# Layer 2's rotary swap by transfers, odd-shaped row writes, a bias on GpSimd, input rows turned first

## The chip, the cores and the metric

The kernel runs on one core of a Trainium2 chip. The metric is the device time of one execution in microseconds. Beside the plain runs one execution was profiled; its trace gives the spans and durations below. Engines: PE is TensorE's matmuls and PEld its weight loads, DVE is VectorE, ACT is ScalarE, POOL is GpSimd, SP is SyncE (here it only issues transfers).

## The reference

A decoder of four layers on x of 128 sequences x 64 tokens x 128 features, float32, residual and layer norm after each block. The seven attention blocks that the change touches have 16 heads of 8 features each; L2's self-attention rotates q and k by halves (feature i is paired with feature i+64):

```python
def _rope(x, base=ROPE_BASE):
    half = D // 2
    x1, x2 = (x[..., :half], x[..., half:])
    return jnp.concatenate([x1 * cos - x2 * sin, x1 * sin + x2 * cos], axis=-1)
# every attention block: softmax(q k / sqrt(8) + mask) v, heads joined, then
# x = layernorm(x + o @ Wo + bo)
```

Between these blocks stand mixtures of experts, a grouped attention, a recurrent block and a channel mix, which the change leaves alone.

## The kernel before

One function, `attention` (line 254), writes seven stages: L0a (self), L0x (cross, rotated by rows), L1x (cross) with L1f (self) behind it, L2a (self) with L2x (cross) behind it, and L3x (cross). A stage that follows another uses its buffers and overlaps its end, so the trace names L1f's tiles L1x and L2x's tiles L2a. The residual rows X stay in SBUF. The work is cut into 32 pairs of tiles (256 rows each).

Each engine has a generator `slot(T)`, one per engine; `all_pairs` (line 156) runs it for T from -4 to 32 and some more, six slots unrolled, 22 in a loop, the rest unrolled. Within an engine the order is the order of the program; between engines `made` waits for a counter. In slot T the stages of work belong to different pairs: scores of T, probabilities and values of T-1, output of T-2, written rows of T-3, projections of T+2, input copy of T+3. L3x, which has a second layer norm in between (`ln_o`), has its output two pairs later.

- TensorE, `slot` at line 620: scores (L563 is the causal mask, L569 the products with KB), the two transposes of the attention output ON (L630), the two transposes of the input rows XS (`fill_turn`, L584), then transposes of the probabilities (L617) in four groups, with the k projection (`fill_projection`, L597, and L599 for the product with the swapped weights) and the q projection between them, the output projection (L672), probabilities times values (L683), and the value projection (`fill_v`, L609). All projections of a slot share the one PSUM bank psF.
- ScalarE, `slot` at line 706: copies the turned output (OT, L711), then the turned input (XT, L719; in L3x CX, L717), the probabilities (PT, L697), the projections (RK through `raw_parts`, L702 to L704, with a bias column; where nothing is rotated QK directly, L736 and L749), then the exponential (L756) and the values (VB, L771).
- VectorE, `slot` at line 777: reduction and subtraction over the scores (L781, L784, 2048 columns each), the normalized rows of pair T-3 into X (L805, one `tensor_scalar` of 128 columns for each of the two tiles; in L3x also OL, L797), the residual sum RB (L816), statistics, 1/sum, and ON (L848). In L0a and L3x it also multiplies the k part by the rotation table (L404).
- GpSimd, `slot` at line 445: the roots of the variances (rs, L459, L461), XR = X + bias row (L482, in the stages with `bias_row`), the copy XS (L498), and at the end the rotation of pair T+2: product with the table (L404), sum of the two parts into KT (L524), the same for q into QT (L529). In L0x its own work is the rotation by rows (L416 to L428), and the bias is added on TensorE (L670, a product of the identity with the broadcast row).
- SP, `slot` at line 349: loads, and four transfers (L385) of the finished keys KT of pair T+2 into KB, after `k_roped`.

For rotation, RK holds for k and for q the projection (columns 0 to 255) and the projection by swapped weights (256 to 511); the product with cosine and sine tables and a sum make the rotated rows. Features are ordered so that the swap by halves is a swap of partitions 0 to 63 with 64 to 127. `pace` adds one to a semaphore that nobody waits for; it is a marker instruction in front of another.

Of the kernel before, what the change touches and what calls it, by code (L numbers as in the profile page):

```python
# [176 lines left out]
def build(nc, io, out):  # L177
    ctx = ExitStack()
    with ctx:
# [74 lines left out]
        def attention(L, q, k, v, o, qs=None, ks=None, bq=None, bqs=None, bk=None, bks=None, bo=None,  # L254
# [5 lines left out]
            turned = ks is not None  # L260
# [13 lines left out]
            RK = mem.sb("RK", [P, 2, 512]) if turned else None  # L274
# [41 lines left out]
            bias_on_pe = by_rows  # L316
            bias_row = rowx[:, 0, :] if ln_o else None if bias_on_pe else bo
# [30 lines left out]
            def sync(sp):  # L348
                def slot(T):
# [29 lines left out]
                    if K.ok:  # L379

                        made(sp, "k_roped" if turned else "o_k", K.p + 1)
                        pace(sp, S)
                        made(sp, "scores", K.p - 1)
                        for b in range(HQ):
                            sp.dma_start(KB[b:P:HQ, K.u, b, :, :].rearrange("p s k -> p (s k)"), KT[b:P:HQ, K.u, :]).then_inc(parity_sem("keys_in", K), 16)  # L385
# [15 lines left out]
            def rope_product(eng, n, tab):  # L401

                parts = RK[:, n].rearrange("p (c s k) -> p c s k", c=2, s=4)
                return eng.tensor_tensor(parts, parts, rope[:, tab:tab + 2, :].unsqueeze(2).to_broadcast([P, 2, 4, SEQ]), ALU.mult)  # L404

            def gpsimd(g):
# [37 lines left out]

                def slot(T):
# [9 lines left out]
                    if F.ok:  # L455

                        made(g, "stats", F.p + 1)
                        made(g, "out_rows", F.p - 1)
                        nc.gpsimd.tensor_tensor(rs[:, F.u, 0, :], mv[:, F.u, :, 1], eps[:, 0:2], ALU.add).then_inc(S["var_eps"].sem, 1)  # L459
                        made(g, "var_eps", F.p + 1)  # L460
                        nc.gpsimd.tensor_tensor(rs[:, F.u, 1, :], rs[:, F.u, 0, :], half[:, 0:2], ALU.pow).then_inc(S["rstd"].sem, 1)  # L461
                        if not rows_on_dve:
                            nc.gpsimd.tensor_tensor(RB[:, F.u], RB[:, F.u], mv[:, F.u, :, 0:1].to_broadcast([P, 2, D]), ALU.subtract).then_inc(S["mix"].sem, 1)
                            made(g, "rstd", F.p + 1)
                            made(g, "mix", F.p + 1)
                            pace(g, S)
                            nc.gpsimd.tensor_tensor(rows_of(F), RB[:, F.u], rs[:, F.u, 1, :].unsqueeze(2).to_broadcast([P, 2, D]), ALU.mult).then_inc(S["out_rows"].sem, 1)
                    A = T - 2
# [47 lines left out]
                    M = T + 2  # L516
                    if turned and M.ok:

                        if not products_on_dve:
                            made(g, "o_k", M.p + 1)  # L520
                            rope_product(nc.gpsimd, 0, ck).then_inc(S["gates"].sem, 1)
                        made(g, "gates", M.p + 1)
                        parity_wait(g, "keys_in", M - 2, 16 * HQ)
                        nc.gpsimd.tensor_tensor(KT[:, M.u], RK[:, 0, 0:256], RK[:, 0, 256:512], ALU.add).then_inc(S["k_roped"].sem, 1)  # L524
                        made(g, "o_q", M.p + 1)
                        rope_product(nc.gpsimd, 1, cq).then_inc(S["gates_out"].sem, 1)
                        made(g, "gates_out", M.p + 1)
                        made(g, "scores", M.p - 1)
                        nc.gpsimd.tensor_tensor(QT[:, M.u], RK[:, 1, 0:256], RK[:, 1, 256:512], ALU.add).then_inc(S["q_roped"].sem, 1)  # L529
# [8 lines left out]
            def tensor(pe):  # L538
# [81 lines left out]
                def slot(T):  # L620
# [3 lines left out]
                    yield  # L624
                    if H.ok:
# [6 lines left out]
                    yield  # L632
                    if N.ok and not by_rows:
                        fill_turn(N)
# [28 lines left out]
                    if H.ok:  # L663
# [5 lines left out]
                        if bias_on_pe:  # L669
                            nc.tensor.matmul(psJ, ident, bo.unsqueeze(1).to_broadcast([P, 2, D]), start=True, stop=False, skip_group_check=True)  # L670
                        for a in range(2):
                            m = nc.tensor.matmul(psJ[:, a, :], OT[:, H.u, a * P:a * P + P], o, start=not bias_on_pe, stop=True, skip_group_check=bias_on_pe)  # L672
# [20 lines left out]
            def scalar(act):  # L693
# [5 lines left out]
                def raw_parts(n, biases):  # L699

                    if biases[0] is None:
                        return nc.scalar.activation(RK[:, n, :], psF[:, :], ACT.Copy)  # L702
                    nc.scalar.activation(RK[:, n, 0:256], psF[:, 0:256], ACT.Identity, bias=biases[0])
                    return nc.scalar.activation(RK[:, n, 256:512], psF[:, 256:512], ACT.Identity, bias=biases[1])  # L704

                def slot(T):
                    A, N, H = T - 1, T + 2, T - 2 - e
                    if H.ok:
                        made(act, "o_turned", H.p + 1)
                        made(act, "proj", H.p - 1)  # L710
                        nc.scalar.activation(OT[:, H.u, :], flat(psOT), ACT.Copy).then_inc(S["ot"].sem, 1)  # L711
                    yield
                    if N.ok and not by_rows:
# [4 lines left out]
                        else:  # L718
                            nc.scalar.activation(XT[:, N.u, :], psF[:, 0:256], ACT.Copy).then_inc(S["o_tx"].sem, 1)  # L719
                    yield  # L720
# [4 lines left out]
                    if N.ok:  # L725
# [5 lines left out]
                        elif turned:  # L731
                            made(act, "k_roped", N.p)
                            raw_parts(0, (bk, bks)).then_inc(S["o_k"].sem, 1)
# [8 lines left out]
                    if N.ok and not by_rows:  # L742
                        made(act, "f_q", N.p + 1)
                        if turned:
                            made(act, "q_roped", N.p)
                            raw_parts(1, (bq, bqs)).then_inc(S["o_q"].sem, 1)
# [29 lines left out]
            def vector(dv):  # L776
                def slot(T):
# [9 lines left out]
                    if turned and products_on_dve and M.ok:  # L787
                        made(dv, "o_k", M.p + 1)
                        rope_product(nc.vector, 0, ck).then_inc(S["gates"].sem, 1)
                    yield  # L790
                    B = T - 3
                    if ln_o and B.ok:
# [3 lines left out]
                        for a in range(2):  # L796
                            m = nc.vector.tensor_scalar(OL[:, B.u, a, :], ON[:, B.u, a, :], mvo[:, B.u, a, 0:1], rso[:, B.u, 1, a:a + 1], ALU.subtract, ALU.mult)  # L797
# [65 lines left out]
            count(dict.fromkeys(("q_roped", "k_roped", "gates_out", "gates"), PAIRS), turned)  # L863
            count(dict(side_made=1, w_in0=32 * PAIRS, w_in1=32 * PAIRS), mask is by_key)
# [1520 lines left out]
        def grouped_attention(later):  # L2385
# [72 lines left out]
            with nc.Block() as block:  # L2458
# [135 lines left out]
                def _(dv):  # L2594
# [78 lines left out]
        turning = attention("L2a", Wm("L2q"), Wm("L2k"), Wm("L2v"), Wm("L2o"), qs=Wm("L2qs"), ks=Wm("L2ks"), bq=C("L2bq"), bqs=C("L2bqs"),  # L2673
                  bk=C("L2bk"), bks=C("L2bks"), bo=rowb[:, 2, :], cq=2, ck=2, mask=static)
# [128 lines left out]
```

## Time and profile before

| | us |
|---|---|
| median of 3 runs | 4016.08 (4015.06 to 4021.43) |
| profiled execution | 4011.83 |
| its span, first to last instruction | 4010.0 |
| PE busy | 3481.2 (87%) |
| DVE busy | 2993.7 (75%) |
| ACT busy | 2291.8 (57%) |
| POOL busy | 1885.8 (47%) |

The shares are averages over stages with different limits; the mean granted TensorE clock is 0.933 of full speed. Attention stages lie at about 12 to 330 us (L0a), 337 to 610 (L0x), 1557 to 2090 (L1x, L1f), 2392 to 2970 (L2a, L2x) and 3521 to 3884 (L3x). In views of waits a row says who waited for whom, the total in us, how often, and the longest. In views in order of time a row has the start, the time to the end, engine, line, operation, output and inputs, the count, and in brackets the idle time before it and who ended that.

### The profile page before, as it was taken

How to read it: one execution, taken by the hardware profiler on the slowest of the kernel's cores; microseconds unless marked ns; L12 is line 12 of the kernel's file. 1: busy time of each engine (PE TensorE's matmuls, PEld its weight loads, DVE VectorE, ACT ScalarE, POOL GpSimd, SP SyncE). 2: the span in 40 equal slices, each digit the busy share in tenths (PEclk: the TensorE clock that was granted, in tenths of full speed). 3: DMA queues.
4: the chain of work that ended last, by engine and by line, in shares of the span. 5: the costliest groups of instructions: out<-in, count | busy, mean ns of one | idle time of the engine just before them, and what ended most of it. 6: DMA issues, size and time to landing. Idle time of an engine off the chain costs nothing. (4 is left out here: it accounts for less than half of the span.)

```text
span 4010.0 us, 127677 instructions
## 1 busy us (share of the span) xinstructions
PE 3481.2 (87%) x46840; PEld 2654.2 (66%) x46840; DVE 2993.7 (75%) x6186; ACT 2291.8 (57%) x3920; POOL 1885.8 (47%) x2970
## 2 busy tenths in 40 slices
PE   8996996797999998999987839999989688879985
PEld 6885775465777776878875627778854254457764
DVE  6986995155898886888863477888867588659975
ACT  5775771344444444778752447777754466556653
POOL 6887864655441111224545436652223355457754
PEclk9997995899999998999986969999989799989988
DMA  2002213697000000110005820001112000000001
GB/s 82 29 27 80 69 54 103 180 262 196 19 16 3 0 0 29 50 49 19 17 19 155 240 70 16 14 25 53 49 42 65 23 0 0 1 26 27 26 8 42
DMA packets 311910, 219.08 MB, mean 55 GB/s; under 512 B 52689, under 2 KB 290257, under 8 KB 311505
## 3 DMA queue, kind: packets, MB, share of 16 engines
q1 hardware_dynamic: 251824, 166.57, 14.3%
q0 software_dynamic: 12288, 25.19, 2.0%
q10 hardware_dynamic: 47520, 23.60, 2.0%
q8 instruction: 177, 2.90, 0.3%
q14 instruction: 101, 0.82, 0.1%
HBM read 131.27 MB, written 54.53 MB: 46 GB/s over the span
## 5 line engine op out<-in xcount | busy, mean ns | idle before, releaser
L781 DVE TENSOR_REDUCE L2a_mx<-L2a_psS 128x32 f32<-128x2048 f32 x64 | 146.7, 2292 | 75.8 <-PE L2a_psS L569 75.8
L781 DVE TENSOR_REDUCE L1x_mx<-L1x_psS 128x32 f32<-128x2048 f32 x64 | 146.7, 2292 | 74.5 <-PE L1x_psS L569 74.5
L2474 POOL TENSOR_TENSOR L1a_rs<-L1a_ag,eps 128x1 f32<-128x1 f32 x64 | 13.0, 204 | 397.8 <-DVE L1a_ag L2639 397.8
L1111 POOL DMA_INDIRECT L0f_sorted_x<-X,L0f_IDX x128 | 123.0, 961 | 93.8 <-DMA L0f_sorted_x<-X,L0f_IDX 35.6
L1530 DVE TENSOR_TENSOR L0f_G<-L0f_SG,L0f_psH 128x512 f32<-128x512 f32 x106 | 73.0, 689 | 120.1 <-ACT L0f_SG L1274 72.7
L459 POOL TENSOR_TENSOR L1x_rs<-L1x_mv,eps 128x2 f32<-128x2 f32 x64 | 12.5, 195 | 310.5 <-DVE L1x_mv L836 310.5
L784 DVE TENSOR_TENSOR L2a_PR<-L2a_psS,L2a_mx 128x2048 f32<-128x2048 f32 x64 | 146.7, 2292 | 7.3
L784 DVE TENSOR_TENSOR L1x_PR<-L1x_psS,L1x_mx 128x2048 f32<-128x2048 f32 x64 | 146.7, 2292 | 7.3 <-DVE L1x_mx L781 0.2
L697 ACT ACTIVATE L2a_PT<-L2a_psP 128x512 f32<-128x512 f32 x256 | 146.0, 598 | 2.9 <-PE L2a_psP L617 1.4
L697 ACT ACTIVATE L1x_PT<-L1x_psP 128x512 f32<-128x512 f32 x256 | 145.9, 595 | 3.0 <-PE L1x_psP L617 1.4
L617 PE MATMUL L1x_psP<-W,L1x_PR 128*128 128x128 f32 x1024 | 146.9, 277 | 0.2
L617 PE MATMUL L2a_psP<-W,L2a_PR 128*128 128x128 f32 x1024 | 145.7, 276 | 0.2
L756 ACT ACTIVATE L1x_PR<-L1x_PR 128x2048 f32<-128x2048 f32 x64 | 122.3, 1912 | 37.0 <-DVE L1x_PR L784 37.0
L2563 PE MATMUL L1a_psO<-rest_WO,L1a_OT 128*64 128x128 f32 x2048 | 125.9, 276 | 11.5 <-ACT L1a_OT L2588 7.4
L756 ACT ACTIVATE L2a_PR<-L2a_PR 128x2048 f32<-128x2048 f32 x64 | 122.6, 1915 | 18.5 <-DVE L2a_PR L784 18.5
L617 PEld LDWEIGHTS L1x_psP<-W,L1x_PR 128*128 128x128 f32 x1024 | 118.0, 142 | 20.7 <-ACT L1x_PT L697 13.9
L617 PEld LDWEIGHTS L2a_psP<-W,L2a_PR 128*128 128x128 f32 x1024 | 120.0, 142 | 17.6 <-ACT L2a_PT L697 7.9
L683 PE MATMUL L1x_psB<-VB,L1x_PT 128*64 128x18 f32 x4096 | 131.4, 212 | 0.0
L2497 PE MATMUL L1a_psF<-L1a_XT,rest_WQ 128*128 128x256 f32 x512 | 131.0, 390 | 0.5 <-DVE L1a_KT L2449 0.5
L2563 PEld LDWEIGHTS L1a_psO<-rest_WO,L1a_OT 128*64 128x64 f32 x2048 | 110.5, 137 | 31.4 <-ACT L1a_OT L2588 31.3
L683 PE MATMUL L2a_psB<-VB,L2a_PT 128*64 128x18 f32 x4096 | 131.2, 212 | 0.0
L683 PEld LDWEIGHTS L1x_psB<-VB,L1x_PT 128*64 128x64 f32 x4096 | 125.0, 138 | 7.8 <-issue 0.4
(624 smaller groups left out, 11625.1 us busy)
## 6 DMA issues: line engine op xcount, KB each, us to landing
L0f_WB<-in_w12a SPq DMA_DIRECT2D x53, 312.0 KB, 3.8
L0f_XB<-L0f_sorted_x SPq DMA_DIRECT2D x53, 256.0 KB, 4.0
L0f_sorted_y<-L0f_YB ACTq DMA_DIRECT2D x53, 256.0 KB, 3.8
L1m_WB<-in_w12b SPq DMA_DIRECT2D x37, 321.0 KB, 4.1
L1m_XB<-L1m_sorted_x SPq DMA_DIRECT2D x37, 256.0 KB, 4.0
L1m_sorted_y<-L1m_YB ACTq DMA_DIRECT2D x37, 256.0 KB, 4.4
L0x_VS<-in_ctx SPq DMA_DIRECT2D x64, 128.0 KB, 2.7
KB<-L1x_QK SPq DMA_DIRECT2D x256, 32.0 KB, 1.8
```

What stands on the lines that cost most here:

```text
L459: nc.gpsimd.tensor_tensor(rs[:, F.u, 0, :], mv[:, F.u, :, 1], eps[:, 0:2], ALU.add).then_inc(S["var_eps"].sem, 1)
L617: m = nc.tensor.transpose(psP[:, bank, n, :], PR[:, A.u, r, b:b + 2, :].rearrange("p h k -> p (h k)"), ident)
L683: m = nc.tensor.matmul(psB[64 * s:64 * s + 64, (j * HP + b) * VW:(j * HP + b + 1) * VW], PT[:, j, b, 64 * s:64 * s + 64], VB[:, A.u, 2 * j ...
L697: nc.scalar.activation(PT[:, j, 4 * hb:4 * hb + 4, :], psP[:, bank], ACT.Copy).then_inc(S["pt_a"].sem, 1)
L756: nc.scalar.activation(PR[:, T.u], PR[:, T.u], ACT.Exp, scale=scale).then_inc(S["probs"].sem, 1)
L781: nc.vector.tensor_reduce(mx[:, T.u, :], sc, AX, ALU.max).then_inc(S["maxed"].sem, 1)
L784: nc.vector.tensor_tensor(PR[:, T.u].rearrange("p r h k -> p (r h) k"), sc, mx[:, T.u, :].unsqueeze(2).to_broadcast([P, 2 * HEADS, SEQ]), ...
L1111: nc.gpsimd.indirect_dma_start(out=sorted_x[p][:, :], out_offset=bass.IndirectOffsetOnAxis(ap=IDX[:, k, t:t + 1], axis=0), in_=X[:, t, :], ...
L1530: nc.vector.tensor_tensor(G[0:f, J % 2, c, :], SG[0:f, c, :], up, ALU.mult).then_inc(S["g_ready"].sem, 1)
L2474: nc.gpsimd.tensor_tensor(rs[:, A.par, 0:1], ag[:, A.par, 1:2], eps[:, 0:1], ALU.add).then_inc(S["var_eps"].sem, 1)
L2497: m = nc.tensor.matmul(bank[:, 256 * j:256 * j + 256], WQ[:, 2 * k + j, :], XT[:, N.u, :], start=True, stop=True)
L2563: m = nc.tensor.matmul(psJ[64 * s:64 * s + 64, :], OT[:, s, c, :], WO[:, s, c, :], start=c == 0, stop=c == QC - 1, skip_group_check=True)
```

## The change

1. L2a is called with `halves=True` and without swapped weights and swapped biases. ScalarE copies only the straight projection (256 columns) of k and of q into RK, which now has two buffers. SP, after both copies, issues two transfers of 64 partitions each that write the swapped halves of k and q together. GpSimd's rotation, now `rotate(M)`, waits for them (`stored`), works on pair T+1 instead of T+2, and stands behind the roots rather than at the end of its slot. SP's key transfers follow it: pair T+1 in L2a, in front of the swap of T+2.
2. The bias of L0x goes from TensorE to XR on GpSimd.
3. In all stages but L0x TensorE does `fill_turn` ahead of the transposes of the output, and ScalarE copies the turned input ahead of OT.
4. Each row write on VectorE (L805, and OL in L3x) becomes two, of columns 0 to 62 and 63 to 127, with an output of 7x9 against an input of 3x21, and 13x5 against 5x13.
5. ScalarE issues a marker (`pace`) in front of the raw copies of L0a, L2a and L3x.

```diff
+                    B = T + ahead if turned else K
+                    if B.ok:
+                        made(sp, "k_roped" if turned else "o_k", B.p + 1)
                         pace(sp, S)
+                        made(sp, "scores", B.p - 1)
                         for b in range(HQ):
+                            sp.dma_start(KB[b:P:HQ, B.u, b, :, :].rearrange("p s k -> p (s k)"), KT[b:P:HQ, B.u, :]).then_inc(parity_sem("keys_in", B), 16)
+                    if halves and K.ok:
+                        made(sp, "o_k", K.p + 1)
+                        pace(sp, S)
+                        made(sp, "o_q", K.p + 1)
+                        for n in range(2):
+                            here, there = slice(64 * n, 64 * n + 64), slice(64 - 64 * n, 128 - 64 * n)
+                            sp.dma_start(RK[here, K.u, :, 256:512], RK[there, K.u, :, 0:256]).then_inc(parity_sem("stored", K), 16)
...
+                def rotate(M):
+                    if turned and M.ok:
+                        if not products_on_dve:
+                            if halves:
+                                parity_wait(g, "stored", M, 32)
+                            else:
+                                made(g, "o_k", M.p + 1)
+                            rope_product(nc.gpsimd, M, 0, ck).then_inc(S["gates"].sem, 1)
+                        made(g, "gates", M.p + 1)
+                        parity_wait(g, "keys_in", M - 2, 16 * HQ)
+                        nc.gpsimd.tensor_tensor(KT[:, M.u], RK[:, kept(M), 0, 0:256], RK[:, kept(M), 0, 256:512], ALU.add).then_inc(S["k_roped"].sem, 1)
...
+                    if halves:
+                        rotate(T + 1)
                     A = T - 2
...
+                    if not halves:
+                        rotate(T + 2)
...
                         scores(T)
                     yield
+                    if N.ok and not by_rows:
+                        fill_turn(N)
+                    yield
                     if H.ok:
...
-                        if bias_on_pe:
-                            nc.tensor.matmul(psJ, ident, bo.unsqueeze(1).to_broadcast([P, 2, D]), start=True, stop=False, skip_group_check=True)
...
+                    if halves:
+                        return nc.scalar.activation(RK[:, N.u, n, 0:256], psF[:, 0:256], ACT.Identity, bias=biases[0])
...
+                def scaled_rows(dst, rows_, mean, root):
+                    for lo, hi, x, y in ((0, 63, 7, 3), (63, D, 13, 5)):
+                        m = nc.vector.tensor_scalar(dst[:, lo:hi].rearrange("p (x y) -> p x y", x=x), rows_[:, lo:hi].rearrange("p (x y) -> p x y", x=y), mean, root, ALU.subtract, ALU.mult)
+                    return m
...
-                            m = nc.vector.tensor_scalar(xo, RB[:, F.u, a, :], mv[:, F.u, a, 0:1], rs[:, F.u, 1, a:a + 1], ALU.subtract, ALU.mult)
+                            m = scaled_rows(xo, RB[:, F.u, a, :], mv[:, F.u, a, 0:1], rs[:, F.u, 1, a:a + 1])
```

## Rows read from the trace of the kernel before

**Rows 1.** Score reductions by tile: count, min/median/max ns, first and last start.

```profile
L781 DVE TENSOR_REDUCE L0a_mx<-L0a_psS x32: 2291/2292/2294, 29.9 to 308.1; 128x32 f32<-128x2048 f32 x32
...
L781 DVE TENSOR_REDUCE L0x_mx<-L0x_psS x32: 2280/2291/2292, 353.0 to 589.7; 128x32 f32<-128x2048 f32 x32
...
L781 DVE TENSOR_REDUCE L1x_mx<-L1x_psS x64: 2291/2292/2294, 1570.7 to 2066.4; 128x32 f32<-128x2048 f32 x64
...
L781 DVE TENSOR_REDUCE L2a_mx<-L2a_psS x64: 2291/2292/2293, 2411.0 to 2946.7; 128x32 f32<-128x2048 f32 x64
...
L781 DVE TENSOR_REDUCE L3x_mx<-L3x_psS x32: 2280/2292/2294, 3542.7 to 3856.2; 128x32 f32<-128x2048 f32 x32
```

**Rows 2.** Windows of L0a, L0x, L3x: us, then PE, PEld, DVE, ACT, POOL busy, clock.

```profile
60.00:290.00 230.00, 225.73 (x4098) 189.44 (x4096) 207.06 (x358) 164.58 (x281) 193.09 (x398) 1.00 0.09 29
380.00:580.00 200.00, 181.78 (x3249) 153.35 (x3247) 194.12 (x288) 149.57 (x235) 173.22 (x306) 1.00 0.23 68
...
3580.00:3830.00 250.00, 237.82 (x3645) 186.35 (x3637) 234.68 (x431) 173.44 (x315) 185.33 (x291) 1.00 0.08 26
```

**Rows 3.** Waits in stretches of L0a, L1f, L3x: total us, times, longest us.

```profile
DVE L0a_mx L781 <- PE L0a_psS L569: 17.3, 25, 0.9
...
DVE L1x_mx L781 <- PE L1x_psS L569: 19.7, 26, 0.8
...
DVE L3x_mx L781 <- PE L3x_psS L569: 12.3, 23, 1.8
```

**Rows 4.** One slot of L2a in order of time.

```profile
2529.97 2.29 DVE L781 TENSOR_REDUCE L2a_mx<-L2a_psS 128x32 f32<-128x2048 f32 x1 [0.87 <-PE L2a_psS L569]
...
2530.32 0.38 ACT L711 ACTIVATE L2a_OT<-L2a_psP 128x256 f32<-128x256 f32 x1 [1.00 <-PE L2a_psP L630]
...
2530.60 0.38 ACT L719 ACTIVATE L2a_XT<-L2a_psF 128x256 f32<-128x256 f32 x1
...
2531.03 0.30 PEld L597 LDWEIGHTS L2a_psF<-L2a_XT,W 128*128 128x128 f32 x2 [0.41 <-ACT L2a_XT L719]
...
2531.57 0.60 PE L599 MATMUL L2a_psF<-L2a_XT,W 128*128 128x256 f32 x2
...
2532.00 1.04 PE L617 MATMUL L2a_psP<-W,L2a_PR 128*128 128x128 f32 x8
...
2533.17 0.30 PEld L597 LDWEIGHTS L2a_psF<-L2a_XT,W 128*128 128x128 f32 x2 [0.37 <-ACT L2a_RK L704]
...
2533.20 1.27 POOL L404 TENSOR_TENSOR L2a_RK<-L2a_RK,rope 128x512 f32<-128x512 f32 x1 [2.32 <-ACT L2a_RK L704]
...
2534.62 1.99 DVE L805 TENSOR_SCALAR X<-L2a_RB,L2a_mv,L2a_rs 128x128 f32 x2
...
2539.31 2.29 DVE L781 TENSOR_REDUCE L2a_mx<-L2a_psS 128x32 f32<-128x2048 f32 x1 [1.04 <-PE L2a_psS L569]
```

**Rows 5.** Transfers of the whole trace: KB each, median us to landing.

```profile
L0x_VS<-in_ctx SPq DMA_DIRECT2D x64, 128.0 KB, 2.7
...
KB<-L2a_QK SPq DMA_DIRECT2D x256, 32.0 KB, 1.8
```

**Rows 6.** VectorE in order of time in L1x: a pair of row writes.

```profile
1702.18 0.60 DVE L805 TENSOR_SCALAR X<-L1x_RB,L1x_mv,L1x_rs 128x128 f32 x2
1702.69 0.42 DVE L816 TENSOR_TENSOR L1x_RB<-L1x_psP,L1x_XR 128x256 f32<-128x256 f32 x1
```

**Rows 7.** Groups of instructions by line and shape: busy us, mean ns.

```profile
L482 POOL TENSOR_TENSOR L2a_XR<-X,rowb 128x256 f32<-128x256 f32 x64 | 47.5, 742 | 0.0
...
L805 DVE TENSOR_SCALAR X<-L3x_RB,L3x_mv,L3x_rs 128x128 f32 x44 | 34.6, 826 | 0.0
L805 DVE TENSOR_SCALAR X<-L0x_RB,L0x_mv,L0x_rs 128x128 f32 x44 | 33.1, 791 | 0.0
...
L797 DVE TENSOR_SCALAR L3x_OL<-L3x_ON,L3x_mvo,L3x_rso 128x128 f32<-128x128 f32 x64 | 31.1, 528 | 2.7 <-POOL L3x_rso L453 2.7
...
L805 DVE TENSOR_SCALAR X<-L0a_RB,L0a_mv,L0a_rs 128x128 f32 x44 | 20.4, 504 | 0.0
```

More of the change, by code:

```diff
@@ L251, in build, with attention @@
         S.advance(dict(zeroed=1))
-        def attention(L, q, k, v, o, qs=None, ks=None, bq=None, bqs=None, bk=None, bks=None, bo=None,
+        def attention(L, q, k, v, o, qs=None, ks=None, bq=None, bqs=None, bk=None, bks=None, bo=None, halves=False,
                       cq=0, ck=0, cross=False, norm=None, mask=None, ln_o=False, affine=None, keep=None, tally=False, arrive=False, tables=None, follows=None):
@@ L259, in attention @@
             by_rows = tables is not None
-            turned = ks is not None
+            turned = ks is not None or halves
+            ahead = 1 if halves else 2
             turn_c = cross and norm is not None and not by_rows
@@ L273, in attention @@
             RA = mem.sb("RA", [P, 2, 2, 2 * P]) if by_rows else None
-            RK = mem.sb("RK", [P, 2, 512]) if turned else None
+            RK = mem.sb("RK", [P, 2, 2, 512]) if turned else None
             QK = mem.sb("QK", [P, 2, 2, 2 * P])
@@ L443, in mean_squares @@
                     nc.gpsimd.tensor_scalar(dst, Q1[:, n, :], 1.0 / HD, RMS_EPS, ALU.mult, ALU.add).then_inc(S[done].sem, 1)
+                def rotate(M):
[10 more added lines that the diff above has]
+                        if halves:
+                            parity_wait(g, "stored", M, 32)
+                        else:
+                            made(g, "o_q", M.p + 1)
+                        rope_product(nc.gpsimd, M, 1, cq).then_inc(S["gates_out"].sem, 1)
+                        made(g, "gates_out", M.p + 1)
+                        made(g, "scores", M.p - 1)
+                        nc.gpsimd.tensor_tensor(QT[:, M.u], RK[:, kept(M), 1, 0:256], RK[:, kept(M), 1, 256:512], ALU.add).then_inc(S["q_roped"].sem, 1)
                 def slot(T):
@@ L515, in slot @@
                         mean_squares(N.p, CS[:, N.u], 0, MC[:, N.u, :], "stat_root", "means")
[L516 to L529, printed above, removed]
+                    if not halves:
+                        rotate(T + 2)
                     Y = T - 4
@@ L668, in slot @@
                             made(pe, "res", H.p)
[L669 to L670 removed]
                         for a in range(2):
[L672 removed]
+                            m = nc.tensor.matmul(psJ[:, a, :], OT[:, H.u, a * P:a * P + P], o, start=True, stop=True)
                         m.then_inc(S["proj"].sem, 1)
@@ L731, in slot @@
                         elif turned:
-                            made(act, "k_roped", N.p)
-                            raw_parts(0, (bk, bks)).then_inc(S["o_k"].sem, 1)
+                            made(act, "k_roped", N.p - 1 if halves else N.p)
+                            pace(act, S)
+                            raw_parts(N, 0, (bk, bks)).then_inc(S["o_k"].sem, 1)
                         else:
@@ L744, in slot @@
                         if turned:
-                            made(act, "q_roped", N.p)
-                            raw_parts(1, (bq, bqs)).then_inc(S["o_q"].sem, 1)
+                            made(act, "q_roped", N.p - 1 if halves else N.p)
+                            pace(act, S)
+                            raw_parts(N, 1, (bq, bqs)).then_inc(S["o_q"].sem, 1)
                         else:
@@ L863, in attention @@
             count(dict.fromkeys(("q_roped", "k_roped", "gates_out", "gates"), PAIRS), turned)
+            count(dict(stored0=16 * PAIRS, stored1=16 * PAIRS), halves)
             count(dict(side_made=1, w_in0=32 * PAIRS, w_in1=32 * PAIRS), mask is by_key)
@@ L2671, in build @@
         keep.close()
-        turning = attention("L2a", Wm("L2q"), Wm("L2k"), Wm("L2v"), Wm("L2o"), qs=Wm("L2qs"), ks=Wm("L2ks"), bq=C("L2bq"), bqs=C("L2bqs"),
-                  bk=C("L2bk"), bks=C("L2bks"), bo=rowb[:, 2, :], cq=2, ck=2, mask=static)
+        turning = attention("L2a", Wm("L2q"), Wm("L2k"), Wm("L2v"), Wm("L2o"), halves=True, bq=C("L2bq"),
+                  bk=C("L2bk"), bo=rowb[:, 2, :], cq=2, ck=2, mask=static)
         run(turning, attention("L2x", Wm("L2xq"), Wm("L2xk"), Wm("L2xv"), Wm("L2xo"), bq=C("L2xbq"), bk=C("L2xbk"), bo=rowb[:, 3, :], cross=True, follows=turning))
```

39 lines of the change are left out of this document (17 added, 22 removed).

## The prediction

> **What bounds the kernel now.** I first read how long one slot (one pair of tiles) takes in each attention stage: the first and the last start of the score reduction, divided by the slots between [rows 1]. L0a 8.97 us, L0x 7.64, L1x with L1f 7.87, L2a with L2x 8.50, L3x 10.11. Next the busy time in a steady stretch [rows 2]: TensorE is busy 225.73 of 230 us in L0a, but 181.78 of 200 in L0x, where VectorE has 194.12. In L3x both are near 94% (237.82 and 234.68 of 250). Then the waits [rows 3]: VectorE's reduction waits for TensorE's scores 17.3 us in 25 slots of L0a (0.69 each), 19.7 in 26 of L1f (0.76), and 12.3 us in about 25 slots of L3x (0.49). So TensorE's program order is the bound in L0a, L1, L2 and L3x, with VectorE 0.5 to 1.0 us behind it, and VectorE is the bound in L0x. The granted clock is 1.00 (2.4 GHz) in these stretches. Last, one slot of L2a in order of time [rows 4]: 9.34 us from one reduction to the next, with two holes in TensorE's weight loads, 0.41 us for the copy of the turned input rows and 0.37 us for the copies of the key halves.
>
> **Layer 2 swap by transfers.** Removed on TensorE, in each of L2a's 32 slots: two projections by swapped weights (ks, qs). One takes 0.43 us of order (L599 starts at 2531.57, the next work at 2532.00) [rows 4], so 0.86. Removed on ScalarE: the second copy of each, which starts the q projection 0.37 us late; with that copy gone the transposes in front (to 2533.04) cover it, so 0.37 more. Added: two transfers of 128 KB each on SP's queue, issued after both copies; in SP's program order they stand behind the four key transfers of the pair before. GpSimd's rotation (product 1.27 us, add about 0.73, twice: 4.0) now waits for these transfers, and runs one slot later and at the head of GpSimd's slot, ahead of the residual's bias add and the input copy. Behind its wait are queued XR (VectorE's residual sum waits for that) and XS. No row shows a partition-crossing swap of this size; the nearest is L0x's pair of 128 KB loads, 2.7 us to landing, and the small end is the key transfers, 1.8 [rows 5]. I take 2.7. Slack, counted from the slot's reduction: the q projection starts at 3.2 today (2533.17), so at 2.0 without those 0.41, 0.43 and 0.37; with its 0.70 and the ScalarE copies in front of its own the q copy ends at about 3.5. I estimate that the next slot's rotation can begin 0.3 before that slot's reduction, so in a slot of P us a swap of up to P-3.8 costs nothing. After the rotation XR ends at -0.3+4.0+0.74 = 4.4; VectorE wants it after its row writes, 4.65 (2534.62) + 1.02 = 5.7: 1.2 more. At P=7.9 the swap may take 5.3. Keys leave at 1.7, land by 4.4, and scores want them some 2 us before the next reduction, at 5.9. So the swap is hidden.
> The Trainium skill, DMA: Bandwidth & Descriptors, Rules for kernel authors, speaks against two transfers to the two halves of the partitions, since they serialize. That would mean double the 1.8 us at worst, an estimate of 3.6, still under 5.3, so the sum would be the same. No run here yet shows it.
>
> **Input rows ahead of the turned output.** In all stages but L0x, TensorE turns the input rows before the attention output, and ScalarE copies them before OT. The order of work is otherwise the same. The hole of 0.41 us exists since ScalarE's OT copy starts at 2530.32 and XT's at 2530.60 [rows 4]; now XT goes first, 0.28 us sooner, and its transpose 0.17 sooner. The k projection gains up to 0.41, at least 0: the copy chain PT, k copy, PT on ScalarE may not follow. What becomes late next is OT, by 0.3 us, wanted by the second group of transposes only. In L0a and L3x a marker instruction is added ahead of each of the two raw copies; no row prices it on ScalarE, I take 0.02 to 0.07 each. I take a net 0.27 a slot for TensorE in L0a and L3x, and let VectorE decide elsewhere. The new order makes the slot's first TensorE work wait for the value copy of the slot before; ScalarE ends that just before today's slots do, so little more than 0.3 can come in L1.
>
> **Odd-shaped writes.** Every row write on VectorE becomes two of 63 and 65 columns with unequal shapes. Today an undisturbed pair of writes costs 0.51 us from start to start (1702.18 to 1702.69) and 0.60 busy; so one takes 0.345 [rows 6]. But the mean is 504 ns in L0a, 791 in L0x, 826 and 528 (OL) in L3x, and 1.99 us for a pair in L2a, where GpSimd's products run beside it [rows 4, 7]. I read the excess as waiting for GpSimd, and take the odd writes to be free of it. I price each odd write like a whole one undisturbed, 0.255 start to start, 1.02 for four, since half of the columns should not cost more than all of them; the upper end is 0.345, the whole busy time of one, 1.38 for four; the lower end is 0.20, if half of the columns save a little.
> The rule for this is in the Trainium skill, VectorE: DVE Perf Modes, What auto-detection actually checks: the two-port mode needs outer dimensions both even or equal, and here they are 3 against 7 and 5 against 13; a half row then has as many steps as a whole row has today, which gives the same 1.02. By its section on the errata each instruction also carries some 150 cycles, an estimate of 0.22 us for 64 columns, 0.89 for four: the sum would be a little better.
>
> **VectorE's need per slot, then.** L0a 8.97-0.69-0.92+1.02 = 8.38 (the pair now is 2x0.504-0.09 of overlap). L0x 7.64-1.49+1.02 = 7.17. L1: 7.87-0.76+0.51 = 7.62. L2a 9.34-1.04-1.91+1.02 = 7.41, where 1.91 is the busy 1.99 less the overlap. L3x 10.11-0.49-2.44+2.04 = 9.22.
>
> **Bias back on GpSimd in L0x.** TensorE loses a product that bounds nothing. GpSimd gains an add of 0.74 us [rows 7]: 173.22/200 of 7.64 is 6.62 busy, 7.36 after it, and with today's small gaps (0.1 to 0.2) 7.5. So L0x changes its bound from VectorE to GpSimd at 7.5, not 7.17.
>
> **The sum**, saving per slot times slots: L0a 0.27x32 = 8.6 (TensorE bound, VectorE below at 8.38). L0x 0.15x32 = 4.8. L1x and L1f 0.17x64 = 10.9 (0.25 by VectorE's 7.62, less since both rings now end within 0.2 us of each other). L2x 0.15x32 = 4.8. L2a: 9.34-0.86-0.37-0.41 = 7.70 at best; L2x takes 7.64 (535.7 less 32 slots of 9.34, over the rest) and lacks the causal mask products, so I take 7.98, 1.36x32 = 43.5, less 3.5 for the longer start-up (one swap of 2.7 and its issue) = 40.0. L3x 0.27x32 = 8.6. Together 77.7. The profiled execution took 4011.8 us (span 4010.0) and would take 3934; the median of the runs is 4.3 us above it, 4016.1, so the forecast is 3938.4.
>
> **Rivals.**
> (A) The odd writes cost 0.34 start to start. For: no row has such a shape, and one write alone is busy for 0.345. Against: back-to-back writes overlap by 0.09 today. VectorE then needs 8.72, 7.51, 7.96, 7.75, 9.90: gains 8.0+4.2-5.8-3.0+40.0+6.4 = 49.8, time 3966.
> (B) The new transfer chain holds L2a at 9.34: only the other 37.7 are left, 3978. For: SP takes both kinds of transfers in order, and three engines pass a pair on. Against: slack of over 2 us above.
> (C) Slower, a late swap. Beyond 5.3 us, L2a's slot is the swap plus 2.6; it eats all gains when the slot is 9.34+37.7/32 = 10.5, a swap of 7.9. At 9 us the slot is 11.6, L2a loses 2.26x32 = 72 where the rest gains 38: 4050. Against: loads of the same size land in 2.7.
> (D) Slower: the odd writes still wait for GpSimd, each as long as a write does today, so it doesn't do what it says. L0x +1.5x32 = 48, L3x VectorE 12.0, +1.9x32 = 60, L0a 9.1, +4.5; L1, L2a and L2x still give 56: +57, 4073. It decides from a mean write of about 0.5 us in L0x and L3x. For: the wait's cause is read from coincidence with GpSimd's work only. Against: L1x, with GpSimd nearly idle, has no excess.
>
> **Chances.** Forecast 0.70, A 0.12, B 0.08, C 0.04, D 0.06. Range: the low end takes every slot at its best, L0a and L3x 0.41, L0x 7.17, L1 and L2x 0.25, L2a 7.70: 13+15+24+49+13 = 114, 3902, say 3903. The high end takes in A and B's figure: 3980. This kernel's measurement can't tell 0.2% (8 us) from no change. Faster is the forecast, A and most of B: 0.88; B and C near their turning point give same 0.03; slower 0.09.
>
> **What would show it.** L2a's slot near 8.0 with no hole before L597; the q copy to rotation path with GpSimd not waiting for DMA. Write durations alike in all stages, near 0.34 busy; if they spread up to 0.8, D. VectorE's wait for scores shrinking to under 0.3 us in L1 shows the second ring; L0x with GpSimd over 95% busy shows its new bound. Wrong would be: a wait of GpSimd's rotation for the swap of over 1 us, or a k projection that still starts 1.2 us after the slot's first transpose.

## The result: slower, 4045.8 us

The changed kernel takes 4045.8 us (median of 4, 4045.1 to 4051.1) beside 4015.6 for the kernel before (median of 4, 4012.5 to 4021.4): a ratio of 1.0076, 95% interval 1.0059 to 1.0094. The forecast was 3938.4, with a range up to 3980. So the sign was wrong, and by sign and mechanism it is rival D: the split writes still wait for GpSimd.

The slots of the five attention stages tell where the time went. The same view as [rows 1], of the kernel after (count, min/median/max ns, first and last start):

```profile
L813 DVE TENSOR_REDUCE L0a_mx<-L0a_psS x32: 2226/2228/2292, 30.6 to 322.6; 128x32 f32<-128x2048 f32 x32
...
L813 DVE TENSOR_REDUCE L0x_mx<-L0x_psS x32: 2278/2290/2292, 368.6 to 640.4; 128x32 f32<-128x2048 f32 x32
...
L813 DVE TENSOR_REDUCE L1x_mx<-L1x_psS x64: 2290/2291/2293, 1624.3 to 2105.6; 128x32 f32<-128x2048 f32 x64
...
L813 DVE TENSOR_REDUCE L2a_mx<-L2a_psS x64: 2290/2291/2293, 2449.1 to 2950.2; 128x32 f32<-128x2048 f32 x64
...
L813 DVE TENSOR_REDUCE L3x_mx<-L3x_psS x32: 2278/2285/2293, 3547.1 to 3888.1; 128x32 f32<-128x2048 f32 x32
```

Last start less first start, over the slots between (31 for 32 reductions, 63 for 64), in us a slot, with the forecast beside it and, already here, the kernel that turned out to matter (the change with the row writes left whole). The forecast column is the slot of before less the saving that the prediction gives the stage:

| stage | before | forecast | after | whole row writes |
|---|---|---|---|---|
| L0a | 8.97 | 8.70 | 9.42 | 8.69 |
| L0x | 7.64 | 7.49 | 8.77 | 7.42 |
| L1x, L1f | 7.87 | 7.70 | 7.64 | 7.63 |
| L2a, L2x | 8.50 | 7.80 | 7.95 | 7.92 |
| L3x | 10.11 | 9.84 | 11.00 | 10.06 |

Times the slots of each stage, after against before: +14.4, +36.2, -14.7, -35.2, +28.5, together +29. Layers 1 and 2 gained 50 us of the 56 forecast for them; L0a, L0x and L3x together lost 79 where 22 of gain was forecast. (These means hold the start of a stage too, and that differs from one profiled execution to the next by 2 or 3 us. Where it matters, the slot in the loop is given beside: the 22 slots between the 7th and the 29th reduction.) Three windows of the kernel after say on which engine (L0a, L0x, L3x; columns as in [rows 2]):

```profile
60.00:290.00 230.00, 212.05 (x3827) 175.22 (x3825) 225.59 (x382) 158.99 (x263) 177.89 (x377) 1.00 0.09 28
400.00:620.00 220.00, 173.52 (x2986) 148.17 (x2983) 215.35 (x323) 143.13 (x221) 182.95 (x320) 0.92 0.20 60
...
3600.00:3850.00 250.00, 219.42 (x3338) 169.22 (x3335) 245.30 (x485) 158.98 (x290) 166.29 (x263) 1.00 0.08 23
```

VectorE, the third busy time, is now at 98% in all three; TensorE fell from 225.73 to 212.05 of 230 in L0a [rows 2]. TensorE now waits for what VectorE hands it; over 3580 to 3830 us of before, the same stage, its weight loads have no wait for VectorE at all. In L3x of after (3600 to 3850; total us, times, longest):

```profile
PEld L3x_psP L641 <- DVE L3x_RB L848: 27.5, 20, 1.4
```

And VectorE spends the time in the row writes. Groups by line and shape, of after (busy us, mean ns):

```profile
L806 DVE TENSOR_SCALAR L3x_OL<-L3x_ON,L3x_mvo,L3x_rso 128x63 f32<-128x63 f32 x64 | 46.5, 727 | 2.7 <-POOL L3x_rso L487 2.7
L806 DVE TENSOR_SCALAR X<-L0x_RB,L0x_mv,L0x_rs 128x63 f32 x44 | 36.8, 837 | 0.0
L806 DVE TENSOR_SCALAR X<-L0a_RB,L0a_mv,L0a_rs 128x63 f32 x44 | 35.6, 808 | 0.0
...
L806 DVE TENSOR_SCALAR X<-L0x_RB,L0x_mv,L0x_rs 128x65 f32 x44 | 30.5, 692 | 0.0
...
L806 DVE TENSOR_SCALAR X<-L1x_RB,L1x_mv,L1x_rs 128x63 f32 x88 | 26.8, 305 | 0.0
```

A write of half a row takes 305 ns in L1x, where GpSimd stands idle beside the writes, but 837 in L0x, where a write of a whole row took 791 [rows 7]. One slot of L0x shows it: the four writes on VectorE, and what GpSimd does beside them (start, busy us).

```profile
505.60 2.72 DVE L806 TENSOR_SCALAR X<-L0x_RB,L0x_mv,L0x_rs 128x63 f32 x4
...
504.69 0.99 POOL L431 TENSOR_TENSOR L0x_RA<-L0x_CS,turn_rows 128x128 f32<-128x128 f32 x2
505.64 1.42 POOL L435 TENSOR_TENSOR L0x_RA<-L0x_RA 128x256 f32<-128x256 f32 x2
507.01 0.68 POOL L441 TENSOR_TENSOR L0x_XS<-L0x_RA,stat 128x256 f32<-128x256 f32 x1
507.61 0.66 POOL L441 TENSOR_TENSOR L0x_CN<-L0x_RA,stat 128x256 f32<-128x256 f32 x1
```

A slot of before has two whole writes, beside GpSimd instructions of the same kind:

```profile
471.94 1.59 DVE L805 TENSOR_SCALAR X<-L0x_RB,L0x_mv,L0x_rs 128x128 f32 x2
```

Four writes in 2.72 us are 0.68 each, and GpSimd's instructions beside them last 0.66 to 0.71 each: every write lasts as long as one GpSimd instruction. The two whole writes took 0.80 each, so twice as many writes wait about twice as often. A possible reason: the diff writes 7x9 against 3x21, but both are 63 neighbouring columns, and both may count as one run of 63. Then the unequal shapes never existed for the chip. The rows can't decide it, since they print only a count of elements ("128x63 f32<-128x63 f32").

**Theory M**: the writes still wait for GpSimd, because touching runs count as one run and the shapes come out equal; shapes that really differ would not wait. **Rival N**: a write waits for GpSimd whatever its shape, so that only the number of writes matters. **Rival O**: the writes are innocent, and the loss comes from another part (transfers, bias, input order, marker). The expectations below call the first half of M, that the split writes still wait, theory W; they call O rival S, and N rival K.

### The profile page after: what moved, and what is told of

It is laid out like the page before. It is cut to its first block and busy times, and to the rows that moved or that the text cites. A ratio compares the mean times of both kernels' runs of the same rounds, so it can differ in the third digit from the quotient of the medians.

```text
span 4043.9 us, 128323 instructions
## 1 busy us (share of the span) xinstructions
PE 3446.5 (85%) x46648; PEld 2629.8 (65%) x46648; DVE 3124.0 (77%) x6698; ACT 2264.9 (56%) x3856; POOL 1899.3 (47%) x3002
## 5 line engine op out<-in xcount | busy, mean ns | idle before, releaser
L705 PEld LDWEIGHTS L2a_psB<-VB,L2a_PT 128*64 128x64 f32 x4096 | 124.6, 138 | 7.8 <-issue 0.2
```

The costliest lines, as they stand in the source:

```text
L705: m = nc.tensor.matmul(psB[64 * s:64 * s + 64, (j * HP + b) * VW:(j * HP + b + 1) * VW], PT[:, j, b, 64 * s:64 * s + 64], VB[:, A.u, 2 * j ...
```

## The experiments

**Only the row writes put back whole.** The change with this edit:

```diff
-m = scaled_rows(xo, RB[:, F.u, a, :], mv[:, F.u, a, 0:1], rs[:, F.u, 1, a:a + 1])
+m = nc.vector.tensor_scalar(xo, RB[:, F.u, a, :], mv[:, F.u, a, 0:1], rs[:, F.u, 1, a:a + 1], ALU.subtract, ALU.mult)
```

(and OL alike).

> The changed kernel with each row write whole again (one write of 128 columns instead of 63 + 65), all else as changed. Theory W: the split writes still wait for GpSimd, so each added write adds a wait, and they cost the whole loss. Then L0a's slot falls from 9.67 to about 8.7, L0x's from 8.9 to about 7.6, L3x's from 11.4 to about 10.0, and the time is about 3945 us, 100 below the changed kernel. Rival S: the split costs only its own busy time and the loss comes from the new order or from GpSimd's bias add; then the time stays above 4020.

Measured: 3949.0 us, ratio to before 0.9835 (0.9819 to 0.9851). It has the lowest median of the study, 67 us below before and 97 below after. O falls: the rest of the change gives most of the forecast gain (67 of 77.7), and the split takes it and 30 us more. The slots are in the table above (the expectation's 9.67, 8.9 and 11.4 for after are slots in the loop; the means are 9.42, 8.77 and 11.00).

**Only the split writes, on the kernel before.** 

```diff
+def scaled_rows(dst, rows_, mean, root):
...
-m = nc.vector.tensor_scalar(xo, RB[:, F.u, a, :], mv[:, F.u, a, 0:1], rs[:, F.u, 1, a:a + 1], ALU.subtract, ALU.mult)
+m = scaled_rows(xo, RB[:, F.u, a, :], mv[:, F.u, a, 0:1], rs[:, F.u, 1, a:a + 1])
```

> The kernel before with only the split row writes. Theory W: L0a, L0x and L3x get slower by 0.7, 1.1 and 1.1 us a slot, together about 95 us: 4110. In L1x the writes are undisturbed and four of them cost about 1.0 us. Rival S: at most 10 us more than before, 4025.

Measured: 4083.7 us, ratio 1.0164 (1.0147 to 1.0181), +67. The expectation said 4110, so W has the sign and some 70% of the size. Slots L0a 9.43, L0x 8.43, L3x 10.98: L0a and L3x land where they do in after, whatever else is in the kernel, with VectorE busy 225.55 of 230 us in L0a. The split costs 67 here and 97 on top of the rest. Of the 30 between them L0a and L3x have 11, where what the other parts give TensorE is lost since VectorE is the bound. The larger share, 18, is L0x's. There the change has only two parts, split and bias: the bias on GpSimd comes with a faster slot for whole writes (7.64 to 7.42) and a slower one for split writes (8.43 to 8.77), as the half writes of 65 columns then take 692 ns in place of 518.

**Shapes that really differ.** The change, with each half write reading its source as runs with a column left out between them, and writing one unbroken run. As written both sides are 3 runs of 21 (5 of 13), equal; only if touching runs are joined do they differ, 3 runs against one. The columns of a row are displaced by this, so the output is another; number and size of all instructions are those of after.

```diff
-for lo, hi, x, y in ((0, 63, 7, 3), (63, D, 13, 5)):
-    m = nc.vector.tensor_scalar(dst[:, lo:hi].rearrange("p (x y) -> p x y", x=x), rows_[:, lo:hi].rearrange("p (x y) -> p x y", x=y), mean, root, ...)
+for lo, hi, x, y, k in ((0, 63, 0, 3, 21), (63, D, 58, 5, 13)):
+    runs = rows_[:, x:x + y * (k + 1)].rearrange("p (x y) -> p x y", x=y)[:, :, 0:k]
+    m = nc.vector.tensor_scalar(dst[:, lo:hi].rearrange("p (x y) -> p x y", x=y), runs, mean, root, ...)
```

> The changed kernel, but each split write reads its columns from runs with a gap between them (3 runs of 21 columns, 22 apart; 5 runs of 13, 14 apart), so that the source cannot be read as one run of 63 or 65 while the destination is one run. Columns land displaced by some places; the amount of work is the same. Theory M: in the changed kernel the trace shows these writes as 128x63 from 128x63, since a shape over columns that touch is one run whatever it is called; equal on both sides, so the writes keep the fast mode that has to wait for GpSimd. Only here source and destination really differ. Then each write takes the same 0.34 us in L0x and L3x as in L1x, none is prolonged, and the slots fall: L0x to about 7.5 (GpSimd), L0a to 8.7, L3x to about 9.8; time about 3950. Rival K: any row write that reads SBUF waits for GpSimd, whatever its shape: then the means stay at 0.5 to 0.84 us in L0x and the time near 4045.

Measured (one execution): 3950.7 us. The groups of the same writes:

```profile
L807 DVE TENSOR_SCALAR X<-L1x_RB,L1x_mv,L1x_rs 128x63 f32 x88 | 28.9, 329 | 0.0
...
L807 DVE TENSOR_SCALAR L3x_OL<-L3x_ON,L3x_mvo,L3x_rso 128x63 f32<-128x63 f32 x64 | 21.1, 330 | 2.7 <-POOL L3x_rso L487 2.7
...
L807 DVE TENSOR_SCALAR X<-L0x_RB,L0x_mv,L0x_rs 128x63 f32 x44 | 14.4, 328 | 0.0
```

And VectorE in one slot of L0x, in order of time:

```profile
480.17 1.07 DVE L807 TENSOR_SCALAR X<-L0x_RB,L0x_mv,L0x_rs 128x63 f32 x4
481.16 0.41 DVE L849 TENSOR_TENSOR L0x_RB<-L0x_psP,L0x_XR 128x256 f32<-128x256 f32 x1
```

Every write takes 328 to 331 ns, in L0x and L3x as in L1x; the four last 0.99 us from start to start in place of 2.61. N falls, and M holds in both its parts: as written the two sides are equal here and unequal in after, and yet it is here that the writes are free, so it is the joined runs that count. What joins them, the tools that build the instruction or the engine, no run shows. That the write runs another way is seen where GpSimd is idle too: 329 ns against 305, for the same 63 columns.

**The control: gaps on both sides alike.** Runs of 20 and 12 columns in source and destination, 3 and 5 of them; 8 columns of each row are left unwritten.

```diff
+for lo, hi, y in ((0, 63, 3), (63, D, 5)):
+    runs = lambda ap: ap[:, lo:hi].rearrange("p (x y) -> p x y", x=y)[:, :, 1:]
+    m = nc.vector.tensor_scalar(runs(dst), runs(rows_), mean, root, ALU.subtract, ALU.mult)
```

> Control for the run before it: gaps on both sides alike (3 runs of 20 columns, 21 apart; 5 runs of 12, 13 apart), so shapes are again equal though not one run; eight columns of a row are left unwritten. Theory M: equal shapes keep the fast mode, so waits for GpSimd are there as in the changed kernel: means of 0.5 to 0.84 us in L0x, time about 4040. If the gaps as such were what frees the writes, they would be as short as with the gapped source alone.

Measured (one execution): 4037.2 us, and the wait is back:

```profile
L807 DVE TENSOR_SCALAR L3x_OL<-L3x_ON,L3x_mvo,L3x_rso 128x60 f32<-128x60 f32 x128 | 70.7, 611 | 2.7 <-POOL L3x_rso L487 2.7
L807 DVE TENSOR_SCALAR X<-L0x_RB,L0x_mv,L0x_rs 128x60 f32 x88 | 61.0, 764 | 0.0
...
L807 DVE TENSOR_SCALAR X<-L1x_RB,L1x_mv,L1x_rs 128x60 f32 x176 | 42.7, 304 | 0.0
```

304 ns without GpSimd, 764 with it. So it is not gaps as such that free a write, but that the two sides differ. The Trainium skill, SBUF — State Buffer, Who interferes with whom, says that VectorE in a two-port mode and GpSimd take turns at a shared pair of ports, each holding it for a whole instruction, and that outside that mode an instruction with one SBUF input does not contend. These two kernels agree with it in both directions, 328 to 331 ns against up to 764.

**Only the swap by transfers, with the marker, on the kernel before.** Bias, input order and row writes stay as before.

```diff
-            RK = mem.sb("RK", [P, 2, 512]) if turned else None
+            RK = mem.sb("RK", [P, 2, 2, 512]) if turned else None
...
+                            sp.dma_start(RK[here, K.u, :, 256:512], RK[there, K.u, :, 0:256]).then_inc(parity_sem("stored", K), 16)
...
+                    if halves:
+                        rotate(T + 1)
...
+                            pace(act, S)
```

> The kernel before with only Layer 2's swap by transfers (and the marker ahead of ScalarE's raw copies). By the prediction's terms without the 0.41 us of the input order: L2a's slot from 9.3 to about 8.3, 32 slots, less 3.5 for the start: about 3985. If the transfers held the slot (rival B) it would stay at 9.3 and the time at 4016.

Measured: 4000.8 us (3986.4 to 4006.2), ratio 0.9956 (0.9936 to 0.9976), 16 us less than before and not the 31 expected. L2a's own slot is as expected, 8.35 for 8.3 (first to 32nd reduction, 2410.2 to 2669.2), but it was 9.23 before and not 9.34 (2411.0 to 2697.0). L2a and L2x together take 8.08 a slot in place of 8.50, -27 us; L3x takes 10.25 in place of 10.11, which the transfers can't explain, as L3x has none.

**Only the marker, on the kernel before.**

```diff
 made(act, "k_roped", N.p)
+pace(act, S)
 raw_parts(0, (bk, bks)).then_inc(S["o_k"].sem, 1)
```

(and ahead of `raw_parts(1, ...)`; it reaches L2a too, not only L0a and L3x.)

> The kernel before with nothing added but the marker instruction ahead of each of the two raw copies of L0a and L3x on ScalarE. It is to say whether the marker is what took L3x's slot from 10.11 to 10.25 us in the run that had the swap by transfers and the marker. If the marker costs 0.02 to 0.07 us each, as the prediction took, and is on TensorE's path through ScalarE: L3x 10.15 to 10.25, L0a 9.01 to 9.11, +3 to +9 us together, 4019 to 4025 beside 4016. If it is hidden: 4016 within 4 us and L3x at 10.1. If it costs over 0.1 each, L3x is over 10.3 and L0a over 9.1, over 4028.

Measured: 4025.9 us beside 4013.9, ratio 1.0031 (1.0020 to 1.0042): +12, over the +3 to +9 that was expected, although by the 95% interval it can be 8. Its profiled execution was the lowest of its eight (4019.7) and shows L3x at 10.21 against 10.11. TensorE's weight loads in L3x, first here and then in before, over the same window:

```profile
PEld L3x_psF L597 <- ACT L3x_RK L704: 9.5, 21, 0.5
```

```profile
PEld L3x_psF L597 <- ACT L3x_RK L704: 7.8, 21, 0.4
```

The q projection comes 1.7/21 = 0.08 us later in each slot, since ScalarE's raw copy ends that much later. In the loop the slots grow by as much in all three stages: L0a 9.03 to 9.12, L2a 9.31 to 9.39, L3x 10.31 to 10.39. Times three stages of 32 slots that is 8 us. (L0a's mean over the whole stage, 8.96 against 8.97, hides it: before lost more at the start.) Set against this kernel rather than against before, the swap alone is worth 25 us by the medians and 30 by the ratios, near the 27 of L2's slots (which have the marker's 3 us in them).

**The same marker, taken out of the fast kernel** (the one with whole row writes):

```diff
-pace(act, S)
 raw_parts(N, 0, (bk, bks)).then_inc(S["o_k"].sem, 1)
...
-pace(act, S)
 raw_parts(N, 1, (bq, bqs)).then_inc(S["o_q"].sem, 1)
```

> The changed kernel with whole row writes and without the marker ahead of ScalarE's raw copies. The run with only the swap had L3x at 10.25 us a slot against 10.11 before, and the marker is the only instruction added there. If the marker costs 0.14 us a slot in L3x, this kernel is 4 to 5 us faster than the one with whole writes alone (3949), so about 3944; if not, equal.

Measured: 3951.8 us (3946.4 to 3966.9), ratio 0.9843 (0.9827 to 0.9860); with the marker it was 3949.0. So in the new order the marker costs nothing that the times can show, although the wait for RK in L3x is 0.44 us a slot with it and 0.35 without, and L3x's slot in the loop 10.16 and 10.11. Why this doesn't reach the time was not isolated. The profiled execution was the slow end of its four, and has L0a at 8.98 where the kernel with the marker has 8.69, and L0x at 7.69 where that has 7.42, although L0x has no marker to take out. So a slot in these stages can fall either way from one execution to the next, and one profile of them should not be read to 0.3 us.

**Only the input order, on the kernel before**: on TensorE `fill_turn` moves ahead of the output's transposes, and on ScalarE the output's copy moves behind that of the turned input.

```diff
                         scores(T)
                     yield
+                    if N.ok and not by_rows:
+                        fill_turn(N)
+                    yield
...
-                    if H.ok:
-                        made(act, "o_turned", H.p + 1)
-                        made(act, "proj", H.p - 1)
-                        nc.scalar.activation(OT[:, H.u, :], flat(psOT), ACT.Copy).then_inc(S["ot"].sem, 1)
-                    yield
```

> The kernel before with only the input rows turned and copied ahead of the turned output. By the prediction TensorE gains 0.27 to 0.41 us a slot in L0a, L2a and L3x, about 0.25 in L1 and L2x, nothing in L0x: 192 slots, about 45 to 55 us, 3965. If the copies on ScalarE or the value copy of the slot before hold TensorE instead, nothing is gained: 4016.

Measured: 3978.1 us, ratio 0.9910 (0.9893 to 0.9926), -39, where 45 to 55 were expected. Slots L0a 8.88, L1 7.61, L2 8.28, L3x 10.02. It is the largest single gain: L1 gives 0.26x64 = 17 us, L2 0.22x64 = 14. L0a gives only 3: its slots are near 8.7 up to the 12th and near 9.2 behind it.

**Only L0x's bias moved to GpSimd, on the kernel before.**

```diff
-bias_on_pe = by_rows
+bias_on_pe = False
```

> The kernel before with only L0x's bias moved to GpSimd. By the prediction VectorE bounds L0x and GpSimd has 7.5 of 7.64 us after the move, so the slot stays at 7.6 and the time within 5 us of 4016. But the run with whole writes had L0x at 7.42 with row writes of 669 ns mean instead of 791: if the move alone shifts GpSimd's work so that the row writes wait less, the slot is 7.4 and the time about 4009.

Measured: 4008.7 us beside 4014.3, ratio 0.9991 (0.9980 to 1.0002): by this run alone it can't be told from no change. The profiled execution (4000.7) was among the fastest of its ten, and has L0x at 7.40.

**The opposite edit on the fast kernel** asks again:

```diff
-bias_row = rowx[:, 0, :] if ln_o else bo
+bias_on_pe = by_rows
+bias_row = rowx[:, 0, :] if ln_o else None if bias_on_pe else bo
```

> The changed kernel with whole row writes and with L0x's bias put back on TensorE, so that only the swap by transfers and the input order are left of the change. Beside the run that keeps the bias on GpSimd (3949 us, L0x 7.42 a slot) it prices the bias on top of the rest. If the bias add on GpSimd is what shortens L0x, by moving GpSimd's products off VectorE's row writes: L0x 7.64 with row writes near 790 ns and GpSimd near 79% busy, so 0.2x32 = 7 us more, 3955 to 3958. If the gain was scatter: L0x 7.4 to 7.5 and 3949 within 4 us. If the parts simply add, the swap's 16 us and the order's 39 from 4016 give 3961.

Measured: 3958.5 us, ratio 0.9858 (0.9842 to 0.9875), against 0.9835 (0.9819 to 0.9851) with the bias on GpSimd; the intervals overlap. The slots of the profiled executions agree in both pairs: L0x 7.64 to 7.40 and 7.63 to 7.42, 0.2x32 = 7 us. First L0x's window with the bias on TensorE, then on GpSimd (both with whole writes, two kernels):

```profile
380.00:560.00 180.00, 162.72 (x2891) 137.35 (x2892) 174.76 (x255) 133.59 (x211) 159.10 (x282) 1.00 0.23 69
```

```profile
380.00:560.00 180.00, 156.81 (x2964) 131.82 (x2968) 175.37 (x271) 138.15 (x218) 177.84 (x314) 1.00 0.24 71
```

GpSimd, the fifth, goes from 88% to 99%, and L0x's write from 806 ns to 669, without a change to it; the likely reason is that GpSimd's products stand elsewhere in the slot. But this gain is not in every execution: the kernel without the marker also has the bias on GpSimd, and its profile has L0x at 7.69 a slot with a mean write of 812 ns. So 7 us is what the move gives when the writes fall well; that it gives it on the whole is not shown. With split writes it is the other way round: 8.43 a slot with the bias on TensorE (the split alone), 8.77 with it on GpSimd.

## Why the prediction was wrong

- **The step that failed**: "I read the excess as waiting for GpSimd, and take the odd writes to be free of it", and the sentence beside it, "here they are 3 against 7 and 5 against 13". The first half was right, the kernel with shapes that really differ confirms it. What failed was the second: it took the diff's rearranged views for the shapes that count, and so took the wait at nothing for the four half writes. The runs show the wait in its place, 0.68 us for each of four writes in L0x in place of 0.255, and 67 us of time for the split alone. The rule cited from the Trainium skill (VectorE: DVE Perf Modes, What auto-detection actually checks) was not at fault: it asks that the outermost dimensions of the two operands be both even or equal, and after joining these are 63 and 63, equal. It was applied to the wrong shapes.
- **The price of a free odd write** was right: 0.255 from start to start, four in 1.02. The kernel with gaps in the source has 0.99.
- **Rival D** had the mechanism, a chance of only 0.06, and sizes that partly cancel, so that its 4073 is not confirmed in its parts: L0x +48 against +36, L3x +60 against +28, L0a +4.5 against +14, layers 1 and 2 -56 against -50. In L3x it took each half write of X to wait like a whole one; they took 518 and 301 ns, 819 together, against 826 for the whole. This fits a wait that is no fixed fee but lasts until the GpSimd instruction under way ends. The argument held against it, that L1x has no excess, was none: L1x says that the wait needs GpSimd, not that the new writes escape it.
- **Layer 2's swap**: 2.7 us to landing was taken, 2.4 measured, less than the 3.6 of the doubling; no run has the swap as one transfer, so what the halves cost is open:

```profile
L2a_RK<-L2a_RK SPq DMA_DIRECT2D x64, 128.0 KB, 2.4
```

The slot was to be 7.98 in L2a; it is 8.35 on the mean of the stage (2449.1 to 2708.1) and 8.21 in the loop, one of them from 2550.81 to 2559.08. And 9.34, from which the saving was counted for all 32 slots, was one slot of the loop; the mean of before is 9.23. The holes foretold to close did close (q projection at 2.23 after the reduction instead of 3.20), but another opened. TensorE's weight loads and matmuls over 2480 to 2640, and GpSimd:

```profile
PEld L2a_psS L587 <- issue: 8.5, 18, 1.5
...
PE L2a_psS L587 <- DMA KB<-L2a_QK: 3.0, 7, 1.2
...
POOL L2a_RK L417 <- DMA L2a_RK<-L2a_RK: 3.7, 5, 1.1
```

The mask products ahead of the scores start late by 8.5/18 = 0.47 us, in 7 slots by up to 1.2 for the key transfers; before, that row had 0.7 us in 4 slots. So the slack of two us in the key path is used up in some slots: a trace of rival B. The third row is the prediction's own sign of being wrong, a wait of the rotation for the swap of over 1 us; it comes in 5 slots, and once at 1.1. L2a gave 0.87x32 = 28 us of the 40.0 forecast, L2x 7.6 (7.81 to 7.57 a slot) where 4.8 was forecast.
- **Input order**: L0a 0.27 forecast, 0.28 with whole writes, in part luck: two other kernels with the new order have 8.88 and 8.98 there. L1 0.17 against 0.24; the prediction took VectorE's need, 7.62, for the bound, but with whole writes, where VectorE needs about 0.5 less, the slot is 7.63 all the same, TensorE is busy 199.36 of 200 us (1820 to 2020) and VectorE waits 0.69 us a slot for scores. So TensorE's order sets it, and the agreement with 7.62 is luck. L3x 0.27 against 0.05, a term mis-sized by 7 us; in the loop it is 0.15 (10.31 to 10.16), and the start of the stage took 2 us back. Where the writes are free VectorE is no bound there (223.29 busy of 250), and the slot is still 10.04. Of its waits, TensorE's weight loads in that kernel:

```profile
PEld L3x_psF L621 <- ACT L3x_RK L728: 11.1, 25, 0.5
...
PEld L3x_psF L621 <- ACT L3x_CX L736: 8.0, 25, 0.5
```

Of the copy of the turned input 0.32 us a slot is still waited for, where before had 13.1/25 = 0.52, and the copy of RK is waited for 0.44 in place of 8.7/24 = 0.36. The step "its transpose 0.17 sooner ... the k projection gains up to 0.41" gave 0.20 and lost 0.08 again, together 0.12, near the 0.15 of the loop. The 0.08 lost is the marker's: with the new order and no marker the wait for RK is 9.0/25 = 0.36 as before. Why the 0.41 hoped for was only 0.20 was not isolated.
- **Bias**: "L0x changes its bound from VectorE to GpSimd at 7.5". For whole writes 7.42 with GpSimd at 99%; but one of the profiles has 7.69 with GpSimd at 95%, so this is right only when the writes fall well.
- **A slip in the sum of VectorE's need in L3x**: 10.11-0.49-2.44+2.04; by the prediction's own terms the two pairs of writes take 2x0.826+2x0.528-2x0.09 = 2.53, not 2.44. It changes no forecast, since TensorE was taken as the bound there.
- **The sum without the writes' share** nearly stands: whole writes give 3949.0 where 3938.4 was forecast, with the misses of L2a and L3x against the gains of L1 and L2x. The forecast's bound for the writes mattered little, since after all other steps TensorE or GpSimd is the bound (3950.7 with really free writes). Even had the odd shapes worked, they would have brought nothing over whole writes that one execution can show. Rival A, odd writes dearer than thought, had looked like the larger risk; the risk in the other direction, that the edit does nothing, was priced but not believed.

## What to carry to other kernels

Before pricing an edit that works through the shape of an access, ask what the instruction holds once neighbouring runs are joined: a rearranged view of touching elements is one run. Where VectorE's short writes wait for GpSimd, count the writes, since each may wait for one GpSimd instruction; don't split one in two unless a trace shows that the halves escape. And if the escape is the aim, first ask whether VectorE is the bound after the other parts of the change: here it wasn't.

## What the runs showed of the hardware

- A half row of 63 columns takes 305 ns when undisturbed, a whole row of 128 takes 340, so half a row saves only 35 ns: by these two, some 270 ns of the time doesn't depend on the columns (an estimate). With shapes that differ the 63 columns take 329 ns, 24 more.
- Waiting writes line up with GpSimd's instructions (0.68 against 0.66 to 0.71 us), so their mean says more of GpSimd's work beside them than of their size: 791 ns for 128 columns and 837 for 63 in L0x.
- The granted clock over 400 to 600 us, in L0x, is 0.91 in after, with TensorE busy 158.56 of 200, and 1.00 with the split writes alone, busy 163.97; with whole writes it is 1.00 too. 0.91 is the mean of a stretch that was partly at the lower of the two levels. What tipped it was not isolated. It didn't set the slot: VectorE is at 98% in both (195.71 and 195.94 of 200), waits for TensorE's scores only 0.4 us in all over 400 to 620 of after, and the 0.47 us by which its slot in the loop is longer (8.97 against 8.50) are about what its four writes take more (0.43).
- The parts do not add: alone they give +67 (split), -39 (order), -16 (swap with marker) and -6 (bias, not clear of zero), together +6, and the whole change measures +30.
